# Layer 1 attention of a four-layer gated decoder: row maxima turned and split on VectorE, one bank job per unit, stores in half as many transfers; waits between the scatters of layer 0

## What is computed

```python
x = x + jnp.tanh(g_ffn[0]) * _L0_ffn_ref(_layernorm(x, axis=-1), ...)
...
q = split_heads(hidden_states @ Wq, q_len)      # with rotary position
scores = jnp.einsum('bhqd,bhkd->bhqk', q, k) * inv_sqrt_d + attention_mask
w = softmax(scores)
attn_output = jnp.einsum('bhqk,bhkd->bhqd', w, v)
a_scores = jnp.tanh(gate) * softmax(jnp.einsum('bhqd,bhkd->bhqk', q, a_k) * inv_sqrt_d)
attn_output = (attn_output + jnp.einsum('bhqk,bhkd->bhqd', a_scores, a_v)) @ Wo
```

## Time and profile before

| | us |
|---|---|
| median of 3 runs (lowest, highest) | 1975.53 (1969.91, 1983.47) |
| the profiled execution | 1976.86 |
| its span | 1975.5 |

### The profile page before, as it was taken

One profiled execution on the slowest core, in us unless ns is written; L12 is line 12 of the kernel. 1 busy time (PEld: TensorE's weight loads), 2 busy tenths in 40 slices (PEclk: granted clock), 3 DMA queues, 4 the chain that ended last, 5 costly groups with the idle time before them and its releaser, 6 DMA issues.

```text
span 1975.5 us, 35976 instructions
## 1 busy us (share of the span) xinstructions
PE 1726.9 (87%) x12221; PEld 1186.7 (60%) x12221; DVE 1330.4 (67%) x4195; ACT 942.1 (48%) x2227; POOL 790.8 (40%) x957
## 2 busy tenths in 40 slices
PE   6888888959897898998896787788999999988998
PEld 2444444636665777777685555455777777766445
DVE  8888873613356887887747888864576676666446
ACT  2666664203323777777644555323444444443352
POOL 3333321264664566564525454211124334433340
PEclk7999999979998999999998899788999999999899
DMA  4444422146963343443123443009100000030767
GB/s 109 102 121 101 95 55 71 36 164 218 299 182 86 82 93 78 87 92 78 32 77 95 145 125 87 18 1 308 46 18 36 32 8 4 13 97 15 232 213 306
DMA packets 180437, 200.41 MB, mean 101 GB/s; under 512 B 86500, under 2 KB 150129, under 8 KB 176928
## 3 DMA queue, kind: packets, MB, share of 16 engines
q1 hardware_dynamic: 161920, 155.92, 29.0%
q0 software_dynamic: 15168, 41.54, 6.2%
q10 hardware_dynamic: 3168, 0.66, 0.2%
HBM read 131.88 MB, written 75.44 MB: 105 GB/s over the span
## 4 chain that ended last, share of the span: by engine, by line
PE 51%; DVE 20%; ACT 10%; issue 7%; POOL 4%; DMA 3%; another core or an unknown queue 2%; ACTq 1%; SPq 1%; DVEq 0%; POOLq 0%
PE psum L3392 3%; PE psum L1052 3%; PE psum L389 3%; PE psum L3466 3%; PE psum L1329 2%; DVE sbuf L539 2%; PE psum L3441 2%; PE psum L352 2%; ACT sbuf L3829 2%; PE psum L3459 2%; PE psum L2278 2%; PE psum L1348 2%; PE psum L1064 2%; PE psum L1764 1%
## 5 line engine op out<-in xcount | busy, mean ns | idle before, releaser
L539 DVE TENSOR_REDUCE sbuf<-psum 128x2 f32<-128x512 f32 x256 | 164.8, 685 | 34.7 <-PE psum L352 33.7
L190 POOL TENSOR_TENSOR sbuf<-sbuf 128x1 f32<-128x1 f32 x128 | 73.5, 576 | 273.4 <-DVE sbuf L182 273.1
L2013 ACT ACTIVATE sbuf<-psum 128x512 f32<-128x512 f32 x256 | 138.4, 594 | 71.6 <-PE psum L1764 67.1
L3829 ACT ACTIVATE sbuf<-psum,sbuf 128x128 f32<-128x128 f32 x256 | 113.7, 455 | 89.2 <-DVE sbuf L3641 89.1
L681 ACT ACTIVATE sbuf<-psum 128x1024 f32<-128x1024 f32 x128 | 130.4, 1021 | 37.5 <-PE psum L374 30.0
L3921 POOL DMA_INDIRECT l_slot_inputs<-sbuf x96 | 97.3, 1014 | 100.7 <-DVE sbuf L3712 75.7
L3466 PE MATMUL psum<-sbuf 128*128 128x256 f32 x512 | 123.8, 385 | 4.9 <-DVE sbuf L3659 4.9
L3392 PE MATMUL psum<-sbuf 128*128 128x256 f32 x512 | 119.4, 388 | 0.8 <-ACT sbuf L3793 0.8
L352 PE MATMUL psum<-sbuf 112*128 112x256 bf16 x512 | 104.0, 288 | 13.1 <-DVE sbuf L539 7.8
L1889 DVE CUSTOM_DVE_ANT_0 sbuf<-psum,sbuf 128x128 f32<-128x128 f32 x512 | 112.5, 284 | 0.5 <-PE psum L1743 0.5
L3392 PEld LDWEIGHTS psum<-sbuf 128*128 128x128 f32 x512 | 98.7, 195 | 21.5 <-issue 8.8
(11 more groups left out here) (436 smaller groups left out, 4501.5 us busy)
## 6 DMA issues: line engine op xcount, KB each, us to landing
l_pair_outputs<-sbuf SPq DMA_DIRECT2D x24, 512.0 KB, 7.0
sbuf<-in_l_gu_pairs SPq DMA_DIRECT2D x32, 384.0 KB, 8.6
sbuf<-l_pair_outputs SPq DMA_DIRECT2D x16, 768.0 KB, 15.9
sbuf<-l_q_parts SPq DMA_DIRECT2D x16, 384.0 KB
l_q_parts<-sbuf SPq DMA_DIRECT2D x64, 96.0 KB, 2.3
sbuf<-l_q_parts SPq DMA_DIRECT2D x32, 192.0 KB
l_k_parts<-sbuf SPq DMA_DIRECT2D x64, 96.0 KB, 2.2
sbuf<-l_k_parts SPq DMA_DIRECT2D x32, 192.0 KB
```

The lines of the kernel that those rows point to most:

```text
L539: dve.tensor_reduce(top3[:, 2 * hp:2 * hp + 2, c], score_bank[v % 2].rearrange("p (j t) -> p j t", j=2), AXX, ALU.max, negate=True).then_i ...
L2013: act.activation(e_t[i % 4][:, h * BANK:(h + 1) * BANK], turn_bank[:, h * BANK:(h + 1) * BANK], ACT.Exp).then_inc(*exped.up())
L3829: last = act.activation(e_t[u % 3][:, j * P:(j + 1) * P], score_bank[:, j * P:(j + 1) * P], ACT.Exp, bias=mt[:, j:j + 1], scale=rq[:, lo + ...
```

## The change

For the row maxima, VectorE turns each 32x32 quarter of the 128x32 maxima into `top_full` (32x128) and makes the three bf16 parts itself, in a chain of four operations, and SP sends them as before. TensorE's, ScalarE's and GpSimd's steps for them are gone. The jobs in the shared bank stand in the even slots alone: adapter keys at 4 instead of 6, values of the odd batch at 6 instead of 7, its output projection at 12 instead of 13, with ScalarE's and GpSimd's steps moved by the same. A store of one kind and batch is one transfer of 128x6x128 instead of two of 128x3x128. In layer 0 every fourth scatter, from the fifth on, waits for one more up product.

```diff
             for b in range(NB):
+                if b % 4 == 0 and (k or b):
+                    pool.wait_ge(*upped.at(LATE - 7 + 4 * k + b // 4))
                 pool_scatter(b, k)
...
     top_full, top_rest = mem.f32(P, H1), mem.f32(P, H1)
-    top_row = [[mem.bf16(P, H1) for _ in range(3)] for _ in range(2)]
+    top_row = [mem.bf16(3 * P, H1).rearrange("h (i t) -> h i t", i=3) for _ in range(2)]
     y_t = mem.f32(D)
...
         last.then_inc(*v_made.up())
-
-    def pe_turn_top(b):
-        pe.wait_ge(*a_maxed.at(4 * b + 4))
-        pe_take_pro(top_kept, b + 1)
-        pe.transpose(pro_bank[0:H1, 0:P], top_t[b % 2], m.ident).then_inc(*top_turned.up())
...
     def pe_pro_slot(g):
-        for at, work in ((-26, pe_adapter_keys), (-24, pe_turn_x), (-22, pe_queries), (-16, pe_keys)):
+        for at, work in ((-28, pe_adapter_keys), (-24, pe_turn_x), (-22, pe_queries), (-16, pe_keys)):
             pair = in_pair(g, at)
...
                 work(pair)
-        for at, i, work in ((-4, 0, pe_turn_top), (-2, 0, pe_values), (4, 1, pe_turn_top), (7, 1, pe_values), (18, 0, pe_project_out), (29, 1, pe_project_out)):
+        for at, i, work in ((-2, 0, pe_values), (6, 1, pe_values), (18, 0, pe_project_out), (28, 1, pe_project_out)):
             pair = in_pair(g, at)
...
         dve.wait_ge(*a_scored.at(n + 1))
-        if s == 0 and b >= 2:
-            dve.wait_ge(*top_turned.at(b - 1))
         dve.tensor_reduce(top_t[b % 2][:, 8 * s:8 * s + 8], split_cols(adapter_bank, 8), AXX, ALU.max, negate=True).then_inc(*a_maxed.up())
+
+    def dve_split_top(b):
+        chain = m.chain
+        hi, mid, lo = (top_row[b % 2][:, i] for i in range(3))
+        dve.wait_ge(*a_maxed.at(4 * b + 4))
+        for c in range(4):
+            last = dve.transpose(top_full[:, 32 * c:32 * c + 32], top_t[b % 2][32 * c:32 * c + 32])
+        last.then_inc(*chain.up())
+        dve.wait_ge(*chain.now())
+        if b >= 2:
+            dve.wait_ge(*top_in[(b - 2) % 3].at(48 * ((b - 2) // 3 + 1)))
+        dve.tensor_copy(hi, top_full).then_inc(*chain.up())
+        dve.wait_ge(*chain.now())
+        dve.tensor_tensor(top_rest, top_full, hi, ALU.subtract).then_inc(*chain.up())
+        dve.wait_ge(*chain.now())
+        dve.tensor_copy(mid, top_rest).then_inc(*chain.up())
+        dve.wait_ge(*chain.now())
+        dve.tensor_tensor(lo, top_rest, mid, ALU.subtract).then_inc(*top_split.up())
...
                 dve_self_scores(u + 2)
+            if 0 <= u + AHEAD < NS and (u + AHEAD) % 4 == 3:
+                dve_split_top((u + AHEAD) // 4)
             dve_pro_slot(2 * u)
...
         if n >= 2:
-            act.wait_ge(*parts_out[n % 2].at(64 * (n // 2)))
+            act.wait_ge(*parts_out[n % 2].at(32 * (n // 2)))
         act.activation(split_cols(part_t[n % 2], 3)[:, 0], val, ACT.Copy).then_inc(*p_hi.up())
...
         act.activation(split_cols(part_t[n % 2], 3)[:, 1], tmp, ACT.Copy).then_inc(*p_mid.up())
-
-    def act_keep_top(b):
-        act.wait_ge(*top_turned.at(b + 1))
-        if b >= 2:
-            act.wait_ge(*top_in[(b - 2) % 3].at(48 * ((b - 2) // 3 + 1)))
-        if b:
-            act.wait_ge(*top_left.at(b))
-        act.activation(top_row[b % 2][0], pro_bank[0:H1, 0:P], ACT.Copy).then_inc(*top_hi.up())
-        act.activation(top_full, pro_bank[0:H1, 0:P], ACT.Copy).then_inc(*top_kept.up())
-
-    def act_mid_top(b):
-        act.wait_ge(*top_left.at(b + 1))
-        act.activation(top_row[b % 2][1], top_rest, ACT.Copy).then_inc(*top_mid.up())
...
     def act_pro_slot(g):
-        for at, work in ((-25, act_keep_adapter), (-23, act_keep_x)):
+        for at, work in ((-27, act_keep_adapter), (-23, act_keep_x)):
             pair = in_pair(g, at)
...
                 work(pair)
-        for i, at in enumerate((-24, -20, -14)):
+        for i, at in enumerate((-26, -20, -14)):
             pair = in_pair(g, at)
...
                 act_mid(3 * pair + i)
-        for at, i, work in ((-3, 0, act_keep_top), (-2, 0, act_mid_top), (-1, 0, act_values), (5, 1, act_keep_top), (6, 1, act_mid_top), (8, 1, act_values),
-                            (19, 0, act_projected), (30, 1, act_projected)):
+        for at, i, work in ((-1, 0, act_values), (7, 1, act_values), (19, 0, act_projected), (29, 1, act_projected)):
             pair = in_pair(g, at)
...
         pool.tensor_tensor(d3, mx.unsqueeze(2).broadcast_to([P, 4, S]), d3, ALU.subtract).then_inc(*shifted_pool.up())
-
-    def pool_rest_top(b):
-        pool.wait_ge(*top_hi.at(b + 1))
-        pool.wait_ge(*top_kept.at(b + 1))
-        pool.tensor_tensor(top_rest, top_full, top_row[b % 2][0], ALU.subtract).then_inc(*top_left.up())
-
-    def pool_lo_top(b):
-        pool.wait_ge(*top_mid.at(b + 1))
-        pool.tensor_tensor(top_row[b % 2][2], top_rest, top_row[b % 2][1], ALU.subtract).then_inc(*top_lo.up())
...
             pool_rotate(pair, k_read, k_roped)
-        for i, at in enumerate((-24, -20, -14)):
+        for i, at in enumerate((-26, -20, -14)):
             pair = in_pair(g, at)
...
                 pool_lo(3 * pair + i)
-        for at, i, work in ((-6, 0, pool_mask), (-3, 0, pool_rest_top), (-2, 0, pool_lo_top), (2, 1, pool_mask), (5, 1, pool_rest_top), (6, 1, pool_lo_top),
-                            (20, 0, pool_add), (31, 1, pool_add)):
+        for at, i, work in ((-6, 0, pool_mask), (2, 1, pool_mask), (20, 0, pool_add), (30, 1, pool_add)):
             pair = in_pair(g, at)
...
         n = 3 * pair + KINDS.index(kind)
-        p5 = part_t[n % 2].rearrange("p (i c b n) -> p i c b n", i=3, c=KD, b=PAIR)
+        p4 = part_t[n % 2].rearrange("p (i b n) -> p i b n", i=3 * KD, b=PAIR)
         sp.wait_ge(*p_lo.at(n + 1))
         for t in range(PAIR):
-            for c in range(KD):
-                dst = parts_dram[kind][pair * PAIR + t, :, c * P:(c + 1) * P, :].rearrange("i r t -> r i t")
-                sp.dma_start(dst, p5[:, :, c, t, :]).then_inc(*parts_out[n % 2].up(16))
+            dst = parts_dram[kind][pair * PAIR + t].rearrange("i (c r) t -> r (i c) t", c=KD)
+            sp.dma_start(dst, p4[:, :, t, :]).then_inc(*parts_out[n % 2].up(16))
...
             sp.wait_ge(*stack_cleared.at(CLEARED[kind, b]))
-        sp.wait_ge(*parts_out[n % 2].at(64 * (n // 2 + 1)))
+        sp.wait_ge(*parts_out[n % 2].at(32 * (n // 2 + 1)))
         for part, cnt, at in TERMS:
...
     def sp_send_top(b):
-        sp.wait_ge(*top_lo.at(b + 1))
+        sp.wait_ge(*top_split.at(b + 1))
         for i in range(3):
-            sp.dma_start(stack_raw["q"][b % 3].bitcast(BF16)[ONES_AT + i:ONES_AT + i + 1, :], top_row[b % 2][i]).then_inc(*top_in[b % 3].up(16))
+            sp.dma_start(stack_raw["q"][b % 3].bitcast(BF16)[ONES_AT + i:ONES_AT + i + 1, :], top_row[b % 2][:, i]).then_inc(*top_in[b % 3].up(16))
...
         for p in range(-1, NPAIR):
```

More of the change, by code:

```diff
@@ L1652, in l1_attention @@
     a_scored, a_maxed = m.mark("a_scored"), m.mark("a_maxed")
-    top_turned, top_hi, top_kept = m.mark("sums_turned"), m.mark("sums_ready"), m.mark("top_kept")
-    top_left, top_mid, top_lo = m.mark("f_u_read"), m.mark("f_scales"), m.mark("f_rounded")
+    top_split = m.mark("sums_ready")
     proj_read = m.mark("proj_read")
```

## The result

The changed kernel takes 1967.2 us, the median of 20 runs (1956.3 to 1981.7), against 1976.6 for the kernel before (20 runs, 1969.9 to 1986.2). The ratio is 0.9946, 95% interval 0.9927 to 0.9966: 9.5 us gained where 30 were forecast. The profiled execution took 1971.0 us (span 1969.7), 5.9 less than that of before.

A forecast was written before the change was run, and what follows sets the result against it. TensorE was taken to bound layer 1, with 4.0 us of holes per pair, and late counts to hold layer 0's expert block. 1976.9 - 17 - 15 = 1944.9, 1944 by the median, rounded to 1946; eight in ten 1929 to 1975.

The forecast's parts named there:

- The waits between the scatters: End of layer 0's expert block: late counts go, first tile at 437 (432 to 443), 12 to 23 us earlier, 15 taken.
- no wait of over 5 us in front of the tanh: Sign of being right: ScalarE's tanhs in the stretch of the scatters show no such wait, with the first expert tile before 443.
- Rival C: Layer 1 gains, but GpSimd waits for late counts between scatters, first tile at about 464: 1971 us, chance 0.12.
- What is given back behind the first tile: Expert tiles of layer 0: some of the 12 to 23 us is lost since fewer weight gathers are issued ahead; 15 kept.
- Row maxima on VectorE: Layer 1's attention: the transposes and split add 1.3 to 2.5 us per batch on VectorE, 1.8 taken, 3.6 per pair.
- Bank jobs apart: Layer 1's shared bank: one TensorE job per unit removes holes of 7.3 + 6.1 = 13.4 us; GpSimd has holes enough.
- the loads were the bound: Sign of being wrong: a layer 1 pair still at 43.9 us with both bank holes gone; the DMA holes' third was wrong.
- sign of over 0.93: Sign of being right: VectorE busy over 0.93 of a pair of batches in layer 1.
- Stores in half as many transfers: Layer 1: SP's issues 1 to 1.5 us shorter; with earlier maxima, TensorE's 7.6 + 6.0 us DMA holes fall by 9.
- D: The counts' lateness goes, but VectorE takes back what layer 1 gains: 1960 us, chance 0.10.
- 17 + 15 us: Layer 1 gains 17 us (7 x 2.5, pair at 41.4); the scatter waits gain 15 us in layer 0.

The follow-up runs named there:

- third kernel: The changed kernel with GpSimd's normalisation of x moved behind the adapter keys' remainder subtraction in the same slot: 1928.8 us, ratio 0.991 to the kernel before.
- reordered version: The changed kernel with GpSimd's normalisation of x behind the adapter keys' remainder: 1928.8 us, ratio 0.991; without the scatter waits 1927.4 us, ratio 0.9931.
- second group: Runs on one other chip, where the kernel before took 1942.9 us; the changed kernel itself took 1944.7 us there, ratio 1.0029.

## Why the prediction was right and wrong

- **The waits between the scatters: right in size up to the first tile; the mechanism fits, as far as the one chip shows it.** Forecast 12 to 23 us earlier to the first tile, 17.2 measured; first tile forecast at 437 (432 to 443), found at 440.8, of which 3.0 us belong to the unchanged start. TensorE was through at 430.9 where 427 was forecast, with the same 3.0 us in it. The sign "no wait of over 5 us in front of the tanh" was put too tight: 4.6 to 5.2 us is the idle time with no count late, and the one wait of 7.21 us holds the 2.6 us by which a count was late. Rival C, GpSimd waiting for counts that stay late, shows for 2.94 us once. That the waits caused the difference is not shown by experiment, since no run of mine met a late count; it rests on the two profiles and their 20 runs.
- **What is given back behind the first tile: under-sized.** I took 3 us of 18 (454.9 to 437, less 15), without working it out. The tile stage got 6.1 us longer, and the stretch behind it 3.5, so 7.6 us are left of the 15. The gathers explain the direction: before, eight of the 39 weight gathers had been issued when the first tile began; after, only four, with a fifth on its way, and 32.7 MB instead of 28.7 move in the tile stage. Busy time of that stage after the change:

```profile
441.00:557.00 116.00, 103.23 (x467) 72.11 (x467) 44.01 (x194) 40.65 (x116) 75.11 (x75) 0.97 0.83 282
```

  At 282 GB/s the 4.0 MB are 14 us of transfer, of which 6.1 show at most. The lower clock at the start of the tiles, shown above, has a share too: TensorE is busy for 103.23 us of this stage, against 101.72 before. How the 6.1 divide between bytes, clock and late counts (below) stays open. Behind the tiles, the kernels with the new split took 46.7 to 50.2 us up to layer 1's first scores and those without it 44.4 to 47.1, so some of the 3.5 belongs to the change; I did not follow it.
- **Row maxima on VectorE: about right.** The four transposes take 0.84 us. From the first transpose to the end of the last subtraction the 16 batches of the changed kernel take 1.96 or 2.33 to 2.36 us, but for the first, which takes 3.69. That is inside the 1.3 to 2.5 and above the 1.8 that I took. A small cause was missed, below.
- **Bank jobs apart: the step that failed.** The two waits of 13.4 us went. But of the adapter keys' earlier slot I wrote that "GpSimd has holes enough". That is a share of busy time over a pair and says nothing about the slot: x's normalisation stands first in that very slot, 2.44 us, and ScalarE's `act_mid` with the exponentials behind it waits for what comes after. The new wait of 15.3 us replaced the 13.4. The sign at the end of the prediction missed this too: the pair still took 44 us with both bank holes gone, and by that sign "the loads were the bound". They were not: the waits for DMAs fell from 13.6 to 8.2 us, and turning GpSimd's order alone, with the loads as they are, freed the pair. The move of a step counts every instruction that it meets in its new place, and I had not listed GpSimd's order there. The third kernel shows it: with only that order turned, the pair takes 41.6 us where my forecast was 41.4, and the version is 13.0 us faster than the kernel before on its chip, 15.5 without the waits (17 were forecast for layer 1). VectorE is then busy for 229.19 of 240 us, 0.95, as the sign of over 0.93 wanted.
- **Stores in half as many transfers: nothing by itself.** SP's issues did fall from 2.13 and 2.99 us to 0.98 and 0.97. TensorE's DMA waits fell by 5.4 us instead of 9.
- **The rivals.** C had the nearest number (1971), by luck: it wanted the first tile at 464 and layer 1's full gain, and neither came. D (1960) was right that the lateness goes and layer 1's gain doesn't show, but it had the wrong engine. The gain was not taken by VectorE's work but by GpSimd's order and ScalarE's queue. Its theory describes what comes next: in the reordered version doubling the split costs 1.7 us a pair.
- **The sum.** Of 17 + 15 us forecast, the profiles show 1.5 + 7.6. So 15.5 us are missing in layer 1 and 7.4 behind the first tile.

The reordered version beats both kernels on its chips: 1928.8 with the scatter waits, 1927.4 without, against 1941.8 and 1942.9. On the chip with late counts it wasn't run. There I would keep its waits. Where nothing is late they cost some 1.2 us up to the first tile, and the two runs of the kernel before with the waits alone are 2.5 and 7.2 us slower by their medians (ratios 1.0022 and 1.0035, the second clear of 1). Where counts were late, the stretch up to the first tile was 17.2 us shorter with them, of which 7.6 were left behind the tiles.

## What to carry to other kernels

When a step is moved to another slot, write down for every engine what stands in that slot, and which instruction of which engine is queued behind the one that will wait; a share of busy time does not answer this. A gain that needs two edits shows with neither alone, so a part that measures zero need not be worthless. Behind waits of 10 and 12 us TensorE ran at the lower clock here, so a wait can cost more than its length (5.1 us on top of 21.8). And a stall whose releaser the trace does not name should be looked for on a second chip before it is priced as a property of the program.

## What the runs showed of the hardware

**Late counts belong to the chip, or to its state at the time, not to the program alone.** The kernel before takes 1976.6 us where the result was taken and 1941 to 1943 on the three numbered chips, 34 us apart. In the profile of the kernel before, where the result was taken, the first tile comes 74.2 us behind the ranks; in all six runs without scatter waits on the three others it comes at 52.7 to 53.1. The expert tiles, the same code, take 110.2 and 116.3 us there and 99.5 to 103.0 on the others, although there too at most six gathers stand ahead of the first tile. The lateness is not confined to the two tanhs: it runs through the tile stage, where GpSimd issues an indirect DMA for every tile and result. The same stage of the changed kernel, by groups of TensorE (busy us, mean ns, idle before), on the result's chip and then on the second group's:

```profile
L1319 PE MATMUL psum<-sbuf 128*128 128x128 f32 x78 | 15.5, 283 | 9.9 <-issue 9.9
L1339 PE MATMUL psum<-sbuf 128*88 128x128 f32 x78 | 15.3, 277 | 9.2 <-DVE sbuf L1397 8.0 <-issue 1.2
```
```profile
L1319 PE MATMUL psum<-sbuf 128*128 128x128 f32 x78 | 15.6, 284 | 7.1 <-DMA sbuf<-l_slot_inputs 7.1
L1339 PE MATMUL psum<-sbuf 128*88 128x128 f32 x78 | 14.9, 273 | 0.1
```

and the waits of GpSimd's gathers (L1487) for counts, on the result's chip:

```profile
POOL sbuf L1487 <- remote: 15.7, 10, 1.6
```

A wait with an unnamed releaser stands nowhere in the tile stage of the other chip. Taken from the starts of single instructions, the tanh of a tile begins 0.04 us behind its up product for all 39 tiles, there and in every other profile from the three chips; on the result's chip, after the change, 9 of 39 begin more than 0.6 us behind it (up to 1.7), and before it 15 of 39 (up to 2.3). What makes the counts late there was not found.

**VectorE stands for GpSimd, casts too.** In the changed kernel, the cast of the split's first part (L1903) took 0.21 us when no GpSimd operation was running or one had at most 0.02 us left, and 0.59 to 0.61 in all six cases in which one had 0.51 to 0.54 us left to run; the second cast took 1.20 us once, with 1.12 left, and the last subtraction 1.03 with 0.88 left. The group means of the changed kernel show it as a first cast dearer than the second, of one shape:

```profile
L1903 DVE CAST sbuf<-sbuf 32x128 bf16<-32x128 f32 x15 | 5.5, 369 | 0.5
L1909 DVE TENSOR_TENSOR sbuf<-sbuf 32x128 bf16<-32x128 f32 x15 | 4.2, 280 | 0.5
L1905 DVE TENSOR_TENSOR sbuf<-sbuf 32x128 f32<-32x128 f32 x15 | 4.2, 280 | 0.5
L1907 DVE CAST sbuf<-sbuf 32x128 bf16<-32x128 f32 x15 | 3.2, 215 | 0.5
```

And the multiplication L1921 took 0.95 us at 741.67, beside GpSimd's L2058 that ended at 742.34, against 0.43 in a stretch without one (at 712.05 of the reordered kernel). The Trainium skill ("SBUF — State Buffer", section "SBUF: two separate sides") names for this lock both a VectorE operation with two SBUF inputs and one in a two-port mode; by that rule the trace agrees, if the casts run in such a mode, which no row shows. The prediction had weighed the rule for the two subtractions, and it was mostly the cast that stood. Its price here was small, 0.15 us a batch (0.369 - 0.215).
